# Mixture attention: head outputs scaled on ScalarE instead of VectorE, and the gates' hits and selection in 16 bits

## What is computed

```python
q = einsum('btc,hdc->bhtd', x, Wq);  k = einsum('btc,hdc->bhtd', x, Wk)
w, sel = top_k(einsum('btc,hec->bthe', x, Ws), 2)          # gate of the values, best 2 of 8
mix_v = einsum('bthk,bthke->bthe', sigmoid(w), one_hot(sel))
v = einsum('bthe,bted->bhtd', mix_v, einsum('btc,edc->bted', x, Wv))
probs = softmax(einsum('bhid,bhjd->bhij', q * scale, k))
attn = einsum('bhij,bhjd->bihd', probs, v)
_, sel_o = top_k(einsum('btc,hec->bthe', x, Wd), 2)         # gate of the outputs, best 2 of 8
mask_o = one_hot(sel_o).sum(axis=3)
res = einsum('bthe,bthd,efd->bthf', mask_o, attn, Wo).sum(axis=2)
```

## Time and profile before

| | |
|---|---|
| median of 3 runs | 1554.07 us |
| lowest and highest | 1545.75 and 1558.92 us |
| the profiled execution: time | 1544.64 us |
| its span (first to last instruction) | 1542.9 us |
| mixture attention in it | about 298 to 810 us |
| granted TensorE clock, mean | 0.878 of 2.4 GHz |

### The profile page before, as it was taken

One profiled execution on the slowest core, in us unless ns is written; L12 is line 12 of the kernel. 1 busy time (PEld: TensorE's weight loads), 2 busy tenths in 40 slices (PEclk: granted clock), 3 DMA queues, 4 the chain that ended last, 5 costly groups with the idle time before them and its releaser, 6 DMA issues. The chain is left out here.

```text
span 1542.9 us, 35004 instructions
## 1 busy us (share of the span) xinstructions
PE 1288.3 (83%) x13602; PEld 1014.9 (66%) x13602; DVE 1185.3 (77%) x2169; ACT 832.8 (54%) x1807; POOL 252.3 (16%) x213
## 2 busy tenths in 40 slices
PE   3399999668898898898957999984229999999997
PEld 2266776446676676676744676753119998989896
DVE  2656777579999999999753777767319999999995
ACT  1256676335565565565533767641117666667673
POOL 2000000000000000000000000001733454545443
PEclk7558788689999999999786999985559999999999
DMA  7000000032524523523410006200647787888771
GB/s 216 11 5 8 5 5 1 1 81 66 138 61 107 135 64 94 142 71 94 118 56 15 6 9 192 68 1 24 254 142 240 227 245 227 250 225 248 224 217 28
DMA packets 196938, 166.70 MB, mean 108 GB/s; under 512 B 72317, under 2 KB 179985, under 8 KB 196801
## 3 DMA queue, kind: packets, MB, share of 16 engines
q1 hardware_dynamic: 177856, 146.67, 31.8%
q0 software_dynamic: 12880, 13.72, 4.1%
q10 hardware_dynamic: 6064, 4.46, 1.0%
HBM read 116.78 MB, written 50.91 MB: 109 GB/s over the span
## 5 line engine op out<-in xcount | busy, mean ns | idle before, releaser
L1782 POOL DMA_INDIRECT out<-m_yo,m_meta x70 | 170.6, 2437 | 229.2 <-DVE m_yo L1900 200.0
L1804 ACT ACTIVATE m_hf<-m_ps,m_bue 128x256 f32<-128x256 f32 x280 | 117.3, 471 | 118.7 <-PE m_ps L84 117.3
L1051 ACT ACTIVATE f_pr<-f_ps,f_nb 128x256 f32<-128x256 f32 x256 | 107.4, 473 | 104.4 <-DVE f_nb L1314 98.9
L82 PE MATMUL m_ps<-m_xt,m_us 128*128 128x256 f16 x560 | 153.2, 274 | 0.0
L83 PE MATMUL m_ps<-m_xt,m_us 128*128 128x256 f16 x560 | 153.1, 273 | 0.0
L84 PE MATMUL m_ps<-m_xt,m_us 128*128 128x256 f16 x560 | 153.1, 273 | 0.0
L82 PE MATMUL m_ps<-m_ds,m_hs 128*128 128x256 f16 x560 | 152.6, 273 | 0.3 <-DVE m_yo L1900 0.3
L83 PE MATMUL m_ps<-m_ds,m_hs 128*128 128x256 f16 x560 | 152.6, 273 | 0.0
L84 PE MATMUL m_ps<-m_ds,m_hs 128*128 128x256 f16 x560 | 152.6, 273 | 0.0
L472 ACT ACTIVATE x_pr<-x_ps,x_mx 128x120 f32<-128x120 f32 x512 | 143.2, 375 | 7.8 <-DVE x_mx L686 7.8
L690 DVE SCALAR_TENSOR_TENSOR x_pt<-x_ps,x_pt 120x512 f16<-120x512 f32 x128 | 88.3, 690 | 73.2 <-ACT x_pt L480 72.5
(11 more groups left out here) (350 smaller groups left out, 3795.5 us busy)
## 6 DMA issues: line engine op xcount, KB each, us to landing
m_uraw<-in_L_ffn_Wup SPq DMA_DIRECT2D x35, 1024.0 KB
m_draw<-in_L_ffn_Wdown SPq DMA_DIRECT2D x35, 1024.0 KB
expert_in<-x_zeros SPq DMA_DIRECT2D x1, 9520.0 KB, 31.2
m_xg<-expert_in SPq DMA_DIRECT2D x35, 256.0 KB, 4.3
head_values<-f_v_row SPq DMA_DIRECT2D x16, 520.0 KB, 5.2
f_vh<-head_values SPq DMA_DIRECT2D x16, 520.0 KB, 3.6
head_outputs<-f_at_row SPq DMA_DIRECT2D x16, 512.0 KB, 2.9
f_at_in_t<-head_outputs SPq DMA_DIRECT2D x16, 512.0 KB, 6.0
```

The source lines that it names most:

```text
L82: pe.matmul(out, lhs[0], rhs[0], start=(n == 0), stop=False)
L1051: ins = act.activation(pr[h % 2][:, ti, :], S(h)[:, ti, :], ACT.Exp, bias=nb[h % 2][:, ti:ti + 1])
L1782: pool.indirect_dma_start(rows_of, bass.IndirectOffsetOnAxis(meta[j % RING][:, ti, 0:1].bitcast(I32), 0), yo[j % 2][:, ti, :], None, bound ...
L1804: ins = act.activation(hf[:, q, m, :], U(q)[:, m, :], ACT.Gelu, bias=weights.bue[par][:, 2 * q + m:2 * q + m + 1], scale=UNSPLIT)
```

## The change

- `normalise` on VectorE becomes `reciprocals`: only the 128x4 reciprocal, which signals a new semaphore `rs_done`. The multiplication goes to ScalarE: a new `normalise` there waits for `rs_done`, and scales each head and tile by itself, four activations of 128x64 (Copy, with a column of the reciprocals as the scale operand), after the exponentials of every odd step. It signals `o_done`.
- `hit`, `sel`, the maximum rank and a copy of the ranks are 16-bit floats; `top` stays 32-bit for the gates' maxima. One instruction at the stage's start makes the 16-bit ranks.

```diff
-        hit = sb("hit", [P, TPB * GATES, E0])
-        sel = sb("sel", [P, TPB, 2, H, E0])
-        top = sb("top", [P, 2, TPB * GATES])
+        hit = sb("hit", [P, TPB * GATES, E0], F16)
+        sel = sb("sel", [P, TPB, 2, H, E0], F16)
+        top, top_rank = sb("top", [P, TPB * GATES]), sb("top_rank", [P, TPB * GATES], F16)
+        rank16 = sb("rank16", [P, E0], F16)
...
+            def normalise(b, hp):
+                h = 2 * hp
+                act.wait_ge(rs_done, H // 2 * b + hp + 1)
+                for i in range(2):
+                    h8, x = at_head(h + i)
+                    for ti in range(TPB):
+                        ins = act.activation(at[:, ti, h8, x, :], O(h)[:, i, ti, 0:DH], ACT.Copy,
+                                             scale=rs[hp % 2][:, 2 * i + ti:2 * i + ti + 1])
+                ins.then_inc(o_done, 1)
...
-                ranks = bcast_mid(s.rank[:, E1 - E0:E1], TPB * GATES)
+                ranks = bcast_mid(rank16[:], TPB * GATES)
...
-                    chain(dve.tensor_tensor(hit[:], g[:], bcast(top[:, 0, :], E0), ALU.is_equal))
+                    chain(dve.tensor_tensor(hit[:], g[:], bcast(top[:], E0), ALU.is_equal))
                     chain(dve.tensor_tensor(hit[:], hit[:], ranks, ALU.mult))
-                    chain(dve.tensor_reduce(top[:, 1, :], hit[:], AX_X, ALU.max))
+                    chain(dve.tensor_reduce(top_rank[:], hit[:], AX_X, ALU.max))
                 elif part == 2:
-                    chain(dve.tensor_tensor(chosen, hit[:], bcast(top[:, 1, :], E0), ALU.is_equal))
+                    chain(dve.tensor_tensor(chosen, hit[:], bcast(top_rank[:], E0), ALU.is_equal))
                     chain(dve.scalar_tensor_tensor(g[:], chosen, MASKED, g[:], ALU.mult, ALU.add))
...
-                chain(dve.reciprocal(r, O(h)[:, :, :, DH]))
-                dve.tensor_tensor(at[:, :, h8:h8 + 2, x, :].rearrange("p t h d -> p t h d"), O(h)[:, :, :, 0:DH],
-                                  r.unsqueeze(3).to_broadcast([P, 2, TPB, DH]), ALU.mult).then_inc(o_done, 1)
+                dve.reciprocal(r, O(h)[:, :, :, DH]).then_inc(rs_done, 1)
```

More of the change, by code:

```diff
@@ L864, in ffn_stage @@
         pv_done = sem("pv_done")
-        o_done = sem("o_done")
+        rs_done, o_done = sem("rs_done"), sem("o_done")
         made = sem("made")
@@ L1080, in _ @@
                         exps(b, h)
+                    if h % 2 == 1:
+                        if h >= 5 and b < B:
+                            normalise(b, (h - 5) // 2)
+                        elif h < 5 and b >= 1:
+                            normalise(b - 1, (h - 5) // 2 + H // 2)
         @block.tensor
@@ L1233, in gate_choice @@
                     chain(dve.reciprocal(mix[:], mix[:]))
-                    chain(dve.tensor_reduce(top[:, 0, :], g[:], AX_X, ALU.max))
+                    chain(dve.tensor_reduce(top[:], g[:], AX_X, ALU.max))
                 elif part == 1:
-                    chain(dve.tensor_tensor(hit[:], g[:], bcast(top[:, 0, :], E0), ALU.is_equal))
+                    chain(dve.tensor_tensor(hit[:], g[:], bcast(top[:], E0), ALU.is_equal))
                     chain(dve.tensor_tensor(hit[:], hit[:], ranks, ALU.mult))
-                    chain(dve.tensor_reduce(top[:, 1, :], hit[:], AX_X, ALU.max))
+                    chain(dve.tensor_reduce(top_rank[:], hit[:], AX_X, ALU.max))
                 elif part == 2:
-                    chain(dve.tensor_tensor(chosen, hit[:], bcast(top[:, 1, :], E0), ALU.is_equal))
+                    chain(dve.tensor_tensor(chosen, hit[:], bcast(top_rank[:], E0), ALU.is_equal))
                     chain(dve.scalar_tensor_tensor(g[:], chosen, MASKED, g[:], ALU.mult, ALU.add))
                 elif part == 3:
-                    chain(dve.tensor_reduce(top[:, 0, :], g[:], AX_X, ALU.max))
-                    chain(dve.tensor_tensor(hit[:], g[:], bcast(top[:, 0, :], E0), ALU.is_equal))
+                    chain(dve.tensor_reduce(top[:], g[:], AX_X, ALU.max))
+                    chain(dve.tensor_tensor(hit[:], g[:], bcast(top[:], E0), ALU.is_equal))
                     chain(dve.tensor_tensor(hit[:], hit[:], ranks, ALU.mult))
                 else:
-                    chain(dve.tensor_reduce(top[:, 1, :], hit[:], AX_X, ALU.max))
-                    chain(dve.tensor_tensor(hit[:], hit[:], bcast(top[:, 1, :], E0), ALU.is_equal))
+                    chain(dve.tensor_reduce(top_rank[:], hit[:], AX_X, ALU.max))
+                    chain(dve.tensor_tensor(hit[:], hit[:], bcast(top_rank[:], E0), ALU.is_equal))
                     chain(dve.tensor_tensor(chosen, chosen, hit[:], ALU.add))
@@ L1320, in pt_part, with reciprocals @@
                                          ALU.mult, ALU.subtract).then_inc(pt_done, 1)
-            def normalise(b, hp):
+            def reciprocals(b, hp):
                 h = 2 * hp
-                h8, x = at_head(h)
                 dve.wait_ge(pv_done, H * b + h + 2)
                 r = rs[hp % 2][:].rearrange("p (h t) -> p h t", h=2)
-                chain(dve.reciprocal(r, O(h)[:, :, :, DH]))
-                dve.tensor_tensor(at[:, :, h8:h8 + 2, x, :].rearrange("p t h d -> p h t d"), O(h)[:, :, :, 0:DH],
-                                  r.unsqueeze(3).to_broadcast([P, 2, TPB, DH]), ALU.mult).then_inc(o_done, 1)
+                dve.reciprocal(r, O(h)[:, :, :, DH]).then_inc(rs_done, 1)
             def back_lo(b, ti):
@@ L1346, in _ @@
             dve.wait_ge(made, 6)
+            chain(dve.tensor_copy(rank16[:], s.rank[:, E1 - E0:E1]))
             for j in range(FF_FRONT - 1):
@@ L1365, in _ @@
                         if h >= 5 and b < B:
-                            normalise(b, (h - 5) // 2)
+                            reciprocals(b, (h - 5) // 2)
                         elif h < 5 and b >= 1:
-                            normalise(b - 1, (h - 5) // 2 + H // 2)
+                            reciprocals(b - 1, (h - 5) // 2 + H // 2)
                     if h == 0 and b < B:
```

## The result

The changed kernel takes 1526.28 us (median of 4 runs, 1525.87 to 1534.32) against 1549.91 us for the kernel before in runs beside it (4 runs, 1540.28 to 1558.92): a ratio of 0.986, 95% interval 0.982 to 0.990. A second series (6 runs against 17) gave 1523.57 against 1547.85 us, 0.984 (0.981 to 0.988). The profiled execution took 1526.24 us (before: 1544.64), its span 1524.5 us (before: 1542.9). It was faster by 1.4%, a little more than the 1% that the prediction calls measurable.

The account below looks back on a forecast made before the run. VectorE paces the mixture attention at 58.9 us per sequence, TensorE 6.5 us behind. Front -0.8, slot 0 -2.8, slots 1 to 6 -21.4, slot 7 +1.0, end +0.5: -23.5 us, so 1530.6 us; 8 in 10 range 1514 to 1547.

Parts of the forecast that it names:

- VectorE paces, TensorE follows: Mixture attention, one sequence of 58.9 us: VectorE busy 56.3 us and pacing, TensorE 6.5 us behind.
- A pair is worth 0.45 us: Reciprocal and product on VectorE take 0.55 us, the lone reciprocal 0.10; each of 64 pairs gives 0.45 us back.
- Three 16-bit instructions at 425 ns, comparisons and reductions as before: Gates on VectorE: two rank products and the selections' sum fall from 692 to 425 ns, 0.8 us per sequence.
- no gain: Rival: 16 bits bring the gates nothing, some 5 us less gained, 1536 us; chance 0.08.
- doubled comparisons: Rival: the two comparisons with a repeated 16-bit operand also run at double rate, 4.3 us more, 1526; chance 0.05.
- The block on ScalarE 0.85 us, 0.93 to its end, hidden but for steps 1, 2 and 10: Four scaling activations behind odd steps' exponentials; VectorE newly waits for f_pt under 1.5 us per sequence.
- Slower, because the block is on the path of each pair: Rival: ScalarE's 0.85 us replaces VectorE's 0.45 in every pair, 19 us slower, 1573 us; chance 0.07.
- TensorE takes back 0.85 us: From step 9 to step 1 of the next slot, TensorE gains 0.95 us where VectorE would gain 1.8.
- Slots 1 to 6, -21.4: Six sequences, each 3.6 us shorter before rounding, a period of 55.3 in place of 58.9 us.
- Front, -0.8: Stage's front: VectorE's gates precede the mixes' DMA, for which it waits 3.83 us; 0.8 us earlier.
- Slot 7 and the end, +1.5: TensorE sets slot 7, so no gain; ScalarE's block adds 1.0 us in its steps and 0.5 at the end.
- The signs: If right: f_xn 55.3 us apart, ScalarE's f_nb waits from 14.5 to about 8 us, TensorE's waits about 3 us.

Follow-up runs that it names:

- gates_only2: The kernel before with only the 16-bit hits, selection and ranks; VectorE keeps the product with the reciprocals: 1537.96 us, ratio 0.994.
- norm_twice: The changed kernel with ScalarE doing each block of four activations twice, first into a spare tile: 1537.08 us, ratio 0.996 to the kernel before.
- lean_after: The changed kernel with the third of three partial products of every score left out on TensorE: 1517.45 us (2 runs), ratio 0.982 to the kernel before.
- pool_split: The changed kernel with GpSimd's low half of the mixes ahead of the mask copies, and the mixes' DMA not waiting for those copies: 1523.12 us, ratio 0.985.

## Why the prediction was right

The forecast was 1530.6 us, 23.5 less than the median then known, 1554.07. The measured medians lie 23.6 apart (1549.91 to 1526.28), with runs that move by more than 10 us. That this is 23.5 almost to the digit is luck: the stage gave 20.6, the term of slots 1 to 6 was too large, the gain in the front did not come, and the term of slot 7 agrees by chance. The mechanism, VectorE pacing and TensorE taking part of the gain back, was right. By its own steps:

- **VectorE paces, TensorE follows**: right. Taking work from TensorE alone gives the kernel before 0.14 us per sequence, taking it from VectorE 3.3.
- **A pair is worth 0.45 us**: 0.47 measured. The lone reciprocal at 524.62 gives way after 0.09 us, where 0.10 was taken.
- **Three 16-bit instructions at 425 ns, comparisons and reductions as before**: right, 425 to 426, 692 and 686 ns, and 0.80 us per sequence in `gates_only2`. The rivals of no gain and of doubled comparisons both fall. By the passage that the prediction cites (the Trainium skill, Vector Engine (DVE) Microarchitecture Reference, section 5.1, Performance modes) an element read 16 times over ran at single rate; here, with 8 repeats, the trace agrees (692 ns).
- **The block on ScalarE 0.85 us, 0.93 to its end, hidden but for steps 1, 2 and 10**: 0.78 to 0.80 to the next start, which is below the 0.81 named as the lower bound, 0.93 to the end, 330 ns each. The wait in step 10 (0.35 against 0.4) was found where it was placed, followed by f_zt. VectorE's waits for f_pt are 1.1 us in three places, under the 1.5 named.
- **Slower, because the block is on the path of each pair**: refuted by `norm_twice`. The advice to multiply on VectorE (the Trainium skill, ScalarE: Activation LUTs, Rules for kernel authors) counts an engine's time rightly (0.8 against 0.47 us), and it is the wrong guide where VectorE is the engine that paces.
- **TensorE takes back 0.85 us**: 0.83 by the step table, in three steps and not only by step 1 as argued: 0.37 in step 10, 0.33 in step 15, 0.13 in step 1. `lean_after` gives 0.57 of it back, 0.12 in step 10 is the block's wait for f_pt, which the prediction took to be wholly hidden, and 0.14 stays open. So the number agrees better than what it was made of.
- **Slots 1 to 6, -21.4**: this term of the sum was too large by 1.7; measured -19.7. The step that failed is "VectorE gains the pairs 5 and 7", in which the pair of step 7 is counted in full. The product's removal brought f_spread_z up against GpSimd's subtraction and 0.47 us per sequence were lost there, 2.8 in six slots; the better pair price gave 0.16 x 6 = 1.0 back. The prediction gave GpSimd a sentence ("hardly any work, 16% busy") and read its busy share, not its place beside VectorE.
- **Front, -0.8**: measured 0.0. VectorE does begin to spread the values 0.6 us earlier in the stage (327.94 - 297.90 = 30.04 us against 30.63), but the first maxima then wait for TensorE. A window of this piece, first of the kernel before, then of the kernel after:

```profile
328.00:338.70 10.70, 6.74 (x120) 5.88 (x120) 7.82 (x9) 2.99 (x5) 0.00 (x0) 0.84 0.21 54
```

```profile
328.00:338.60 10.60, 8.02 (x120) 7.02 (x120) 7.87 (x10) 2.99 (x5) 0.00 (x0) 0.60 0.18 52
```

  The same 120 products took 6.74 us at a granted clock of 0.84 and 8.02 us at 0.60. That the clock took the 0.6 us is read from these rows. `pool_split` supports the other half of it: there VectorE spreads 1.4 us earlier than in the kernel after, and the first maxima still wait for TensorE. With fronts of 39.6 and 40.7 us for the same instructions, one profile of each kernel could not have shown 0.8 us anyway.
- **Slot 7 and the end, +1.5**: measured +1.8, and that is luck. The prediction charged ScalarE's block (+1.0 in the steps, +0.5 at the end). `gates_only2` has no block and takes the same 68.9 us at the same granted clock, 0.73, so the 1.5 us of the two terms together are not seen in any run; what the rows show is the clock, 0.77 before and 0.73 after.
- **The signs**: f_xn 55.6 apart in place of 55.3. ScalarE's waits for f_nb fell to 10.2 us, not to about 8, and TensorE's were 4.6 + 0.4 = 5.0 us, not about 3. The prediction shows no working for either number. The sequence got shorter by 3.3 us while ScalarE has 5.9 us more to do, so its idle time fell by 9.3 us, but only 4.3 of this are waits for f_nb; its waits for TensorE fell by most of the rest. TensorE's busy time fell as well, from 52.3 to 50.5 us in the windows, whose clock was 0.97 and is 1.00, which leaves only 1.5 us for its waits.

## What to carry to other kernels

When one engine paces and another idles, price a moved instruction by the distance of starts on the pacing engine and look only at the places where it will be waited for: 0.8 us on ScalarE bought 0.47 on VectorE at a cost near zero. Then step through the sequence once with every start moved up, and look at what the pacing engine's two-source SBUF instructions now run beside on GpSimd, however idle GpSimd is on average. A table of the distances between one recurring instruction's starts, step by step, shows at once which gains came through and which did not. Before a difference of 1 or 2 us in one part of a profile is explained, compare that part in two kernels that run the same instructions there.

## What the runs showed of the hardware

- A VectorE instruction with two SBUF sources that began while GpSimd read SBUF lasted longer by what was left of GpSimd's instruction, less 0.12 to 0.14 us, in six places: 1.71 us in place of 1.21 with 0.62 us left, 1.34 with 0.27 left, 2.50 in place of 0.69 with 1.95 left. A one-source GpSimd copy did it as well as a subtraction.
- It goes both ways: a GpSimd copy that began 0.10 us behind VectorE's spreading took 1.29 us in place of 0.29, and VectorE took 1.23 for its usual 1.21.
- On VectorE a product or sum of 128x512 from SBUF takes 425 ns with all operands 16-bit and 692 ns in 32 bits; a 16-bit comparison whose second operand repeats one number 8 times along the row stays at 692, and a 16-bit reduction at 686.
- Four activations of 128x64 out of PSUM with a column as scale take 0.93 us, 0.78 to 0.80 to the next start, so 0.2 us each, although each is recorded as 330 ns.
- Slot 7 and the end, with the same instructions, took 66.9 us at a mean granted clock of 0.77 and 68.9 at 0.73; in part of slot 7 it stood at 0.50, or 1.2 GHz.
